# A DLRM tower with a compressed interaction network: products in PSUM, a stacked half tile in layer 0, low parts and gathers in another order

## What is computed

```python
e = jnp.stack([tbl_f[ids[:, f]] for f in range(39)], axis=1)     # (512, 39, 16), shortened
x0 = xk = e
for idx, (W, b) in enumerate([(w0, b0), (w1, b1), (w2, b2)]):     # W: (39, fields of xk, 128)
    z = jnp.einsum('bhd,bkd,hks->bsd', x0, xk, W) + b[None, :, None]
    z = jax.nn.relu(z)
    if idx != 2:
        xk = z[:, :64, :]; direct.append(z[:, 64:, :])
    else:
        direct.append(z)
z = jnp.sum(jnp.concatenate(direct, axis=1), axis=-1)             # (512, 256)
h = jnp.concatenate([z, dense_ctx], axis=1)
h = jnp.maximum(h @ W_top1 + b_top1, 0.0)                         # 272 -> 512
h = jnp.maximum(h @ W_top2 + b_top2, 0.0)                         # 512 -> 256
y = h @ W_top3                                                    # 256 -> 1
```

## Time and profile before

| what | value |
|---|---|
| median of 3 runs | 666.9 us (666.8 to 668.03) |
| the profiled execution | 669.69 us |
| its span, first to last instruction | 667.9 us, mean granted clock 0.995 |
| TensorE matmul busy | 625.5 us (94%) |
| DVE busy | 577.0 us (86%), 507 instructions |
| ACT busy | 283.8 us (42%) |
| POOL busy | 463.2 us (69%): low parts 265.0 (x112), gathers 197.5 (x160) |
| DMA | 98.19 MB, mean 147 GB/s |

### The profile page before, as it was taken

The page is one execution under the profiler, slowest core; times in us unless marked ns, Lnnn a source line. Parts: engine busy times, 40 slices in busy tenths (PEclk is TensorE's granted clock), DMA queues, the critical chain, the costliest instruction groups (busy, mean ns, idle before and its releaser), DMA issues.

```text
span 667.9 us, 7153 instructions
## 1 busy us (share of the span) xinstructions
PE 625.5 (94%) x1916; PEld 358.0 (54%) x1916; DVE 577.0 (86%) x507; ACT 283.8 (42%) x341; POOL 463.2 (69%) x277
## 2 busy tenths in 40 slices
PE   0367999999999999999999999999999999999998
PEld 0124555565555555565655555555656555555553
DVE  4138899999999999999999999999999999999670
ACT  3004443544454444534454444444444544445323
POOL 6507768686887878786977878786878878716340
PEclk9997999999999999999999999999999999999999
DMA  6879586694939486785939495875939395862000
GB/s 226 186 189 222 118 202 133 149 199 93 217 84 227 94 195 139 174 174 117 221 80 216 82 218 114 189 159 135 212 93 216 77 225 105 199 131 67 0 1 0
DMA packets 27902, 98.19 MB, mean 147 GB/s; under 512 B 7473, under 2 KB 16433, under 8 KB 19826
## 3 DMA queue, kind: packets, MB, share of 16 engines
q1 hardware_dynamic: 20137, 90.92, 61.1%
q10 hardware_dynamic: 2633, 5.82, 3.0%
q0 software_dynamic: 5120, 1.32, 1.9%
HBM read 94.20 MB, written 3.84 MB: 147 GB/s over the span
## 4 chain that ended last, share of the span: by engine, by line
PE 85%; DVE 5%; DMA 3%; POOL 3%; issue 2%; ACT 1%; ACTq 0%; DVEq 0%; SPq 0%; POOLq 0%
PE z L527 40%; PE z L538 13%; PE z L533 12%; PE z L535 11%; PE z L518 4%; DVE products L405 4%; DMA x_rep<-x_rows 2%; PE z L521 2%; POOL gathered L361 1%; POOL low L309 1%; PE z L520 1%; PE spare L571 1%; PE z L595 1%; DVE low L309 1%; PE xk L595 1%
## 5 line engine op out<-in xcount | busy, mean ns | idle before, releaser
L405 DVE TENSOR_TENSOR products<-x_rep,xk 128x1024 f32<-128x1024 f32 (+1 forms) x288 | 366.7, 1333 | 28.1 <-ACT xk L621 27.2
L309 POOL TENSOR_TENSOR low<-products,high 128x1024 fp32r<-128x1024 f32 x112 | 265.0, 2391 | 134.2 <-ACT high L637 92.9
L527 PE MATMUL z<-products,w_whole 128*128 128x512 f32 x672 | 313.4, 599 | 0.0
L637 ACT ACTIVATE high<-products 128x1024 fp32r<-128x1024 f32 x176 | 184.3, 1056 | 243.0 <-DVE products L405 200.6
L361 POOL DMA_INDIRECT gathered<-in_tables,rows_sb x160 | 197.5, 1235 | 46.5 <-issue 44.2
L533 PE MATMUL z<-high,w_high 128*128 128x512 f32 x352 | 188.2, 535 | 16.5 <-ACT high L637 16.5
L527 PEld LDWEIGHTS z<-products,w_whole 128*128 128x128 f32 x672 | 128.6, 191 | 113.1 <-issue 98.3
L535 PE MATMUL z<-high,w_low 128*128 128x512 f32 x352 | 139.6, 397 | 0.0
L538 PE MATMUL z<-low,w_high 128*128 128x512 f32 x352 | 114.0, 405 | 4.3 <-DVE low L309 3.6
L533 PEld LDWEIGHTS z<-high,w_high 128*128 128x128 f32 x352 | 66.9, 190 | 62.3 <-issue 33.2
L309 DVE TENSOR_TENSOR low<-products,high 128x1024 fp32r<-128x1024 f32 x64 | 93.8, 1467 | 1.3 <-ACT high L637 1.3
(11 more groups left out here) (34 smaller groups left out, 102.8 us busy)
## 6 DMA issues: line engine op xcount, KB each, us to landing
x_rep<-x_rows SPq DMA_DIRECT2D x60, 768.0 KB, 16.4
x_rep<-x_rows SPq DMA_DIRECT2D x61, 512.0 KB, 9.3
x_rows<-gathered SPq DMA_DIRECT2D x15, 225.0 KB
x_rep<-in_w ACTq DMA_DIRECT2D x2, 1280.0 KB, 9.4
gathered<-in_tables,rows_sb POOLq DMA_INDIRECT x160
x_rep<-x_rows SPq DMA_DIRECT2D x4, 384.0 KB, 12.6
x_rep<-x_rows ACTq DMA_DIRECT2D x4, 384.0 KB, 19.0
x_same<-x_rows SPq DMA_DIRECT2D x15, 90.0 KB
```

What stands on the lines that cost most here:

```text
L309: ops.tensor_tensor(low[0:p, slot, 0:n, :], products[0:p, index % RING, 0:n, :], high[0:p, slot, 0:n, :].bitcast(fp32), ALU.subtract).then ...
L405: nc.vector.tensor_tensor(slots, rep, row.unsqueeze(1).broadcast_to([p, n, N]), ALU.mult).then_inc(made, 1 + pair)
L527: mm = nc.tensor.matmul(out, w_whole[0:p, at, i, :], products[0:p, slot, i, :], start=(t + i == 0), stop=(t + i == tiles[layer] - 1))
L637: nc.scalar.activation(high[0:p, slot, 0:n, :], products[0:p, index % RING, 0:n, :], ACT.Copy).then_inc(rounded, 1)
```

## The change

- **Letters.** `KINDS` goes from layer 1 "pwppwpwddh", layer 0 "dwww", layer 2 "wdwpwpwpwh" to "wpwpwppwdh", "wsdw", "wwpwpdpwph": eight groups a chunk with POOL's low part instead of seven, three with DVE's instead of four.
- **A stacked half tile in layer 0.** New anchors and a turned order of the second half's rows (`TURNED`, `row_of`) let the seventh tile hold its pairs in 64 partitions. It is a group of its own, letter "s" (`ALONE`), the second of layer 0: ACT rounds it, DVE makes its low part, both lie in `stacks`, TensorE does only the two stacked passes.
- **PSUM.** The products of "d" groups go to `d_products` (two banks) and not into the ring; the ring counts only the others (`RINGED`). `x0_same` has one buffer; ACT copies it to a PSUM bank `x0_bank` (`copy_same`) at index 2 of the body, and layer 0's products read that. The three spare banks are gone.
- **The end.** With the spare banks go the early dense products and their loads; all four are now made after layer 1 of the last chunk. The hidden layers use other banks.
- **Lag and places.** `LOW_LAG` is 1; ahead of a "d" product all outstanding low parts of DVE are made. `after_layer2` is called at index 3 (was 4), `after_layer1` at index 13 (was 12), `after_layer0` and the reduction of `logits01` at index 17 (was 18).
- **Gathers.** One of the ten is issued behind index 1, nine behind index 6 (`GATHERS`), instead of ten ahead of index 10.
- **Waits for parts.** `parts_new` waits for exactly the parts of `x0_rep` that a group is the first to read.

```diff
-ANCHORS = [(0, F, 0), (F, HALF - F, F - 2 * T0), (HALF, 19, 6), (HALF + 19, 45, 32)]
+TURNED = 5
+ANCHORS = [(0, 34, 12), (34, 30, 14), (HALF, 9, 5), (73, 6, 6), (79, F, 1), (118, 10, 31)]
+def row_of(e, t):
+    return T1 + (t + TURNED) % (T1 - 1) if e else t
...
-KINDS = {1: "pwppwpwddh", 0: "dwww", 2: "wdwpwpwpwh"}
+ALONE = "one tile of 64 partitions, split and stacked"
+KINDS = {1: "wpwpwppwdh", 0: "wsdw", 2: "wwpwpdpwph"}
...
+RINGED = [i for i, g in enumerate(BODY) if g[4] != LOW_DVE]
 RING = 8
...
-LOW_LAG = 2
+GATHERS = {1: 1, 6: 9}
+LOW_LAG = 1
...
-        x0_same = sb("x0_same", [128, 2, N])
+        x0_same = sb("x0_same", [128, N])
...
-        spare = [bank("spare0"), bank("spare1"), bank("spare2")]
-        z_hidden1 = [spare[0], spare[1], spare[2], z[0]]
-        z_hidden2 = [z[1], xk[0]]
+        x0_bank = bank("x0_bank")
+        d_products = ctx.enter_context(nc.psum_tensor("d_products", [128, 2, N], fp32))
+        z_hidden1 = [x0_bank, z[0], xk[0], z[1]]
+        z_hidden2 = [d_products[:, 0, :], d_products[:, 1, :]]
...
+        def product(index, p, n):
+            if index in RINGED:
+                return products[0:p, RINGED.index(index) % RING, 0:n, :]
+            return d_products[0:p, 0:n, :]
...
-                    if index == N1 and c + 2 < C:
-                        gather(c + 2)
                     if BODY[index][4] == LOW_POOL and not (c == C - 1 and index in LAYER0):
                         low_part(pool, nc.gpsimd, c, index)
+                    if index in GATHERS and c + 2 < C:
+                        if sent == 0:
+                            pool.wait_ge(x0_written, 16 * WRITES * (c + 1))
+                        for j in range(sent, sent + GATHERS[index]):
+                            gather(c + 2, j)
+                        sent += GATHERS[index]
...
-                    row = x0_same[0:p, bass.ds(half, 1), :].rearrange("p a n -> p (a n)")
+                    row = x0_bank[0:p, :]
...
+                    if kind == LOW_DVE:
+                        while late:
+                            make_low(c, late.pop(0))
...
-            for m in range(EARLY):
-                nc.tensor.matmul(z_hidden1[m][:, :], early_wt1d[:, m * 128:(m + 1) * 128], early_dense,
-                                 start=True, stop=False)
...
             for m in range(H1 // 128):
+                if z_hidden1[m] is z[1]:
+                    pe.wait_ge(direct1_ready, C)
+                nc.tensor.matmul(z_hidden1[m][:, :], wt1d_sb[:, m * 128:(m + 1) * 128], dense_sb,
+                                 start=True, stop=False)
                 add_logits(m, 0, logit01, before_last)
                 add_logits(m, 1, logit2, before_last)
...
+            def copy_same(c):
+                act.wait_ge(same_loaded, 16 * len(ANCHORS) * (c + 1))
+                if not (isinstance(c, int) and c == 0):
+                    act.wait_ge(made, count("all", c - 2, N1 + N0 - 1))
+                nc.scalar.activation(x0_bank[:, :], x0_same[:, :], ACT.Copy).then_inc(x0_ready, 1)
...
-                    if index == 4 and not first:
+                    if index == 2 and not last:
+                        copy_same(c + 1)
+                    if index == 3 and not first:
                         after_layer2(c - 1, first=isinstance(c, int) and c == 1)
-                    if index == N1 + 2:
+                    if index == N1 + 3:
                         after_layer1(c)
-                    if index == N1 + N0 + 4 and not last:
+                    if index == N1 + N0 + 3 and not last:
                         after_layer0(c)
```

More of the change, by code:

```diff
@@ L45, in pairs_of_layer0 @@
     for t in range(T0):
-        for p in range(S):
+        for p in range(S if t < T0 - 1 else HALF):
             pair = frozenset((anchor_of(p), field_of(p, t)))
@@ L54, with parts_new @@
 FIRST_PARTS = [(0, 2), (2, 4), (4, T0), (T0, 10), (10, 14), (14, 17), (17, T1)]
-def part_of(t):
-    return next(q for q, (first, end) in enumerate(PARTS) if first <= t < end)
+assert all(row_of(1, end - 1) - row_of(1, first) == end - 1 - first for first, end in PARTS)
+def parts_new(index, parts):
+    layer, t, n = BODY[index][:3]
+    if index in PAIRED:
+        n += BODY[index + 1][2]
+    before = {u for i in range(STARTS[layer], index) for u in range(BODY[i][1], BODY[i][1] + BODY[i][2])}
+    return [q for q, (first, end) in enumerate(parts)
+            if before.isdisjoint(range(first, end)) and not set(range(t, t + n)).isdisjoint(range(first, end))]
 DENSE = 16
@@ L80, in groups_of @@
     for letter in KINDS[layer]:
+        if letter == "s":
+            found.append((layer, tiles - 1, 1, partitions[-1:], ALONE))
+            tiles -= 1
+            continue
         n = min(2, tiles - t)
@@ L103 @@
 PAIRED = [0,2]
-assert all(i % 2 == 0 and BODY[i][:1] == BODY[i + 1][:1] and BODY[i][3] == BODY[i + 1][3] for i in PAIRED)
-LOW_LAG = 2
+assert all(RINGED.index(i) % 2 == 0 and RINGED.index(i + 1) == RINGED.index(i) + 1 for i in PAIRED)
+assert all(BODY[i][:1] == BODY[i + 1][:1] and BODY[i][3] == BODY[i + 1][3] for i in PAIRED)
+GATHERS = {1: 1, 6: 9}
+assert sum(GATHERS.values()) == GB
+LOW_LAG = 1
 COUNTED = {
@@ L308, in low_part @@
             slot = part_slot(index)
[L309 removed]
+            ops.tensor_tensor(low[0:p, slot, 0:n, :], product(index, p, n),
                               high[0:p, slot, 0:n, :].bitcast(fp32), ALU.subtract).then_inc(low_by[kind], 1)
@@ L378, in _ @@
             pool.wait_ge(rows_made, 1)
-            gather(0)
-            gather(1)
+            for c in range(2):
+                for j in range(GB):
+                    gather(c, j)
             for index in LAYER0:
@@ L509, in _ @@
         def _(pe):
-            tiles = [T0, T1, T1]
             def contract(c, index):
                 layer, t, n, partitions, kind = BODY[index]
-                slot, out = index % RING, z[layer][:, :]
-                if kind == STACKED:
-                    at, stack = WHOLES.index(index), STACKS.index(index)
-                    pe.wait_ge(made, count("all", c, index))
-                    nc.tensor.matmul(out, w_whole[:, at, 0, :], products[:, slot, 0, :], start=False, stop=False)
+                out = z[layer][:, :]
+                first, last = index == STARTS[layer], index == ENDS[layer]
+                if kind in (STACKED, ALONE):
+                    stack = STACKS.index(index)
+                    if kind == STACKED:
+                        pe.wait_ge(made, count("all", c, index))
+                        nc.tensor.matmul(out, w_whole[:, WHOLES.index(index), 0, :], product(index, 128, 1)[:, 0, :],
+                                         start=False, stop=False)
                     pe.wait_ge(stack_low, count("stacked", c, index))
-                    nc.tensor.matmul(out, w_stack_high[:, stack, :], stacks[:, stack, :], start=False, stop=False)
+                    nc.tensor.matmul(out, w_stack_high[:, stack, :], stacks[:, stack, :], start=first, stop=False)
                     mm = nc.tensor.matmul(out, w_stack_low[:, stack, :], stacks[0:HALF, stack, :],
-                                          start=False, stop=True)
+                                          start=False, stop=last)
                 elif kind == WHOLE:
@@ L526, in contract @@
                     for i, p in enumerate(partitions):
-                        mm = nc.tensor.matmul(out, w_whole[0:p, at, i, :], products[0:p, slot, i, :],
-                                              start=(t + i == 0), stop=(t + i == tiles[layer] - 1))
+                        mm = nc.tensor.matmul(out, w_whole[0:p, at, i, :], product(index, p, n)[:, i, :],
+                                              start=(first and i == 0), stop=(last and i == n - 1))
                 else:
@@ L538, in contract @@
                         mm = nc.tensor.matmul(out, w_high[0:p, at, i, :], low[0:p, part, i, :],
-                                              start=False, stop=(t + i == tiles[layer] - 1))
+                                              start=False, stop=(last and i == n - 1))
                 mm.then_inc(used, 1)
@@ L576, in _ @@
             pe.wait_ge(direct0_ready, C)
-            for m in range(EARLY, H1 // 128):
-                nc.tensor.matmul(z_hidden1[m][:, :], wt1d_sb[:, m * 128:(m + 1) * 128], dense_sb,
-                                 start=True, stop=False)
             pe.wait_ge(logit01_ready, C - 1)
```

131 lines of the change are left out of this document (66 added, 65 removed).

## The result

The changed kernel takes 685.5 us (683.67 to 687.26) where the kernel before takes 667.2 in the same comparison: ratio 1.027 [1.0247, 1.0302]. Slower, as forecast, but by 18 us and not by 7, and outside the range. (A ratio counts only the executions within 1.5% of the fastest of their kernel, which matters for `both_undone` alone.) The profiled execution took 683.67 us, its span is 681.9 against 667.9: 14.0 us more. Cut at ACT's first relu of `xk[1]` (the two rows out of layer 1, 64x512) in chunk 0 and in chunk 15, the 14.0 are +0.6 at the start (73.45 to 74.08), +10.0 in the fifteen turns between (557.3 to 567.3) and +3.4 at the end (37.1 to 40.5). The sum had -1.0, +4.9 and +2.9.

A forecast was written before the change was run, and what follows sets the result against it. The loop over POOL's port lock and the gather was to lengthen chunks beyond TensorE's 36.7 us of work. Start -1.0, turns +4.9 and end +2.9 made +6.8, added to the median 666.9: 673.7 us, range 663.0 to 679.0.

The forecast's parts named there:

- The sum: Whole kernel: start -1.0, fifteen turns +4.9, end +2.9, together +6.8 us on the median 666.9.
- Bound and prices: Each chunk: TensorE's floor 36.75 us; DVE low parts from PSUM 1.22, products with PSUM operands no dearer.
- Rival E: DVE beside POOL: PSUM operand does not free POOL's port, DVE late by 2 us a chunk, near 695; chance 0.03.
- The lock: Layer 2's end: POOL's low part starts before DVE's stack low part, which ends 0.55 after it; layer 1 starts 1.16 later.
- Rival B: Loop has slack, TensorE is the bound, for instance DVE taking the port before POOL: 663.4 us; chance 0.21.
- Lock and gather together: Layer 1: late start plus a 1.39 us gather between POOL's low parts, stalls 0.84; chunk 37.55 instead of 37.12.
- The step that failed: Layer 2: ACT's rounding of "d" comes after layer 0's relus and another rounding, 0.15 us late, between 0 and 0.3.
- Rival C: Nine gathers stretched as now, layer 2's first POOL low part late: about 0.5 us a chunk more, 680; chance 0.08.
- Start: Chunk 0: layer 1 begins when the double product is made, not with ACT's rounding: -1.0 us, between -2 and +3.
- End: After the last layer 1: three more dense products on TensorE's path, +3.1, last layer 2 0.3 shorter: +2.8 to +2.9 us.

The follow-up runs named there:

- both_undone: Changed kernel with POOL's last layer 2 low part waiting for the stack's low part, and all ten gathers behind layer 1's fourth low part: median 678.1 us, ratio 1.006.
- before_relus_earlier: Kernel before, with ACT's relus of layer 0 and DVE's reduction of `logits01` one group earlier in layer 2: 678.2 us, ratio 1.012.
- no_gathers: Changed kernel without the gathers of chunks 2 to 15, all chunks reading the rows gathered for chunks 0 and 1: 671.9 us, ratio 1.004.
- gather_sweep: both_undone plus a POOL memset ahead of each chunk's gathers, 96 columns longer in each chunk, so they end later: one execution, 676.3 us.
- POOL's wait alone: Changed kernel with POOL's last low part of layer 2 waiting until DVE has made the stack's low part: 669.0 us, ratio 0.999.

## Why the prediction was right or wrong

**Bound and prices: right.** TensorE's floor was put at 36.75 and is 36.67. PSUM operands cost nothing on DVE, against the 62 cycles more that the Trainium skill has for a PSUM source (VectorE: DVE Perf Modes, the TRN2 errata): 1221 and 1217 beside 1214. Rival E is out.

**The lock: right.** 2.52 beside POOL's 2.38, the end 0.55 behind POOL's, and 0.69 where POOL is made to wait. DVE's low part from PSUM takes 1.23 beside POOL's at 463.50 and 236.67 above, so it isn't held up. The Trainium skill (SBUF — State Buffer, "SBUF: two separate sides") calls the shared port pair an exclusive lock held for the whole instruction, and these rows agree. Rival B, that DVE takes the port first, did not happen in the changed kernel; it is seen in four turns of the kernel with the relus behind "d", at 36.5 to 36.7.

**Lock and gather together: right in sum, partly by luck.** 37.55 was forecast, nine turns have 37.54 to 37.63. The split was off, and the two errors cancel: the lock alone costs 0.3 above the floor, not nothing, and the gather 0.6, not 0.8. The gather takes 1.13 between two low parts (477.29 to 478.42), where I had 1.39.

**The step that failed** is "ACT reaches its rounding only after layer 0's relus (...) and one other rounding: 0.15 late, between 0 and 0.3". The 2.0 us of the relus were counted, but their start was taken from the moment when TensorE is done. The earlier trace rows show the relu at 452.12, t = 5.73, with no wait in brackets, some 1.3 after TensorE's end of layer 0. That row shows that ACT was late; it cannot show when the signal came. In the kernel before the signal was in time, at 5.85 after the `xk[1]` relu in every turn, and it stays so with the relus one group earlier (`before_relus_earlier`). What makes it late is the change's new place for the gathers, whose last one ends at 6.1 and not at 8.0: without gathers (`no_gathers`) no signal is late, and with the last one put off to 6.75 (`gather_sweep`) they are in time again. The change also moves ACT to the moment of the signal, and there the wait is bare: 0 to 0.35 in ten turns, 1.0 to 1.8 in the other five. Both the value and its upper bound were too small.

In the sum: four turns in the middle are 0.6, 1.3, 1.3 and 0.6 above 37.6, and the one before the last, forecast at 36.8, took 37.75 with the relu at 7.03 (37.18 in the two other traces of this kernel, with the relu in time). That is 3.8 and 0.6, together 4.4 of the 5.1 that the turns have more than forecast; 0.4 is that turn of 37.18 itself, where the lock alone was priced at nothing. Nothing else is long in these turns. The price of the late signal is shown by `both_undone` against the run that differs from it only in the relus' place: 566.5 and 550.1. Rival C had the gathers to blame, but in another way: they were to be stretched. They are not (mean 990 ns, before 1235), and POOL's first low part of layer 2 was in time.

This step is the largest single miss, but not all of it. The forecast of +6.8 on this comparison's 667.2 is 674.0, and 685.5 was measured, 11.4 more: 5.1 are the turns (4.4 of them the late signal), 1.6 the start, 0.5 the end, and 4.2 lie between the profiled executions and the medians.

**Start: open.** Forecast -1.0, in this trace +0.6. Eleven traces of kernels that share the changed start have the first `xk[1]` relu at 70.9 to 74.6, mean 73.5; the two with the start of before have it at 73.45 and 74.44, and the one without the early dense products at 74.78. The scatter of 3.7 is larger than the term, so neither its sign nor its size is shown.

**End: mechanism right, size 0.5 short.** Forecast +2.9, measured +3.4 without a dip of the clock. The four dense blocks take 641.25 to 652.59, 11.3 against 7.6 in the earlier trace rows: 3.7, not 3.1. Each of the four now changes from the passes over 16 rows to those over 128 and back:

```profile
641.25 1.12 PE L618 MATMUL x_bank<-x_rep 16*128 16x512 f32 x2
642.30 1.88 PE L607 MATMUL x_bank<-logit,x_rep 128*128 128x480 f32 x4
644.11 1.12 PE L618 MATMUL z<-x_rep 16*128 16x512 f32 x2
```

Each block is 2.86 from start to start, where in the earlier trace rows the same product takes 1.05 and sixteen 480-column rows 6.54 in one go, 1.64 for four. The kernel before with the products late, where they stay together, has 2.6 for the three. That the changes are the reason is what these lengths suggest; no run tried it alone.

**Between profile and comparison.** The spans are 14 us apart, the medians 18. The profiled execution of the kernel before, 669.69, lies 2.4 above its median in this comparison, and that of the changed kernel, the fastest of its four, 1.8 below: that is the 4.2. The 18 is itself on the high side: beside the kernel before at 668.6, the two further runs of the changed kernel took 684.1 and 684.2, some 15.5 more (ratios 1.020 and 1.021). The executions of the changed kernel differ in the number of late signals (turns of 567.3, 568.5 and 569.0 in its three traces) and in a dip of the clock at the end (40.5, 42.2 and 42.1).

## What to carry to other kernels

A row without a wait proves that the engine was late, not that its input was early, and least of all that it will be early once other work is moved: before an operation is moved up against the end of another engine's work, ask how much later than that end its signal may come, and keep the operation where something covers it if work that is needed soon is queued behind it. A small operation that shares a port with a long one may be worth an explicit order: 0.7 us of DVE ahead of 2.4 us of POOL, by one wait, took the changed kernel from 684 to 669 us here, part of it because the opened loop absorbs late signals. And a change that loses may be one move away from one that wins, if its parts are undone singly.

## What the runs showed of the hardware

- The signal of TensorE's last group of a layer can come up to 2.3 us late while GpSimd ends a run of indirect gathers (chunk 6 of the sweep: increment at 8.18 after the `xk[1]` relu, 5.86 in a turn in time). It was never late without gathers (15 turns), nor in the kernel before with the relus one group earlier, where the gathers of 13 turns run until 8.0. In the sweep it was late in all six chunks whose last gather ended 5.9 to 6.2 after the relu of layer 1, with TensorE done at 5.85, in time in the seven where it ended at 6.75 or later (one by 0.3 late), and in time at 4.66. The edges are not the same everywhere: with POOL's wait alone it was in time with an end at 5.5 (once 0.2 late), and 0.75 late with one at 4.9; in the changed kernel, at 6.1, it is sometimes late and sometimes not.
- The late signal does not go with late matmuls: they start on time, and the next group's increment, due 1.7 us later, follows 0.06 behind the late one (7.72 and 7.79 in the long turn of the changed kernel, 8.18 and 8.24 in chunk 6 of the sweep). So increments seem to be held up and then let go together. Why stays open: SP's write of the gathered rows starts at 7.4 to 7.6 in good and in long turns of the changed kernel alike, so it doesn't set the time.
- ACT rounds 1024 columns out of PSUM in 1021 ns (L672, `d_products`) and out of SBUF in 1057.
- In the kernel with ten gathers in a block the granted clock was 0.58 of the upper level in 658 to 662 us, and the next dense layer took 8.8 us instead of 7.1. In the changed kernel it stayed at 1.00 there in one trace and fell to 0.62 and 0.64 in the two others. TensorE had waited the same 0.5 us for DVE's last reduction ahead of it in the kernel with ten gathers and in the first trace of the changed one. So the end of this program has two lengths, 1.7 us apart.
